# The first layer's output stage: one plain fp32 product in place of three fp32r passes

## What is computed

```python
rw = _gating(hidden_states, sim_matrix, gates)            # (4, 2048, 16)
q, k, v = ...                                             # weighed by rw, head width 64
attn = jnp.einsum('bqk,bkd->bqd', jax.nn.softmax(scores, axis=-1), v)
mixed = attn[:, :, None, :] * rw[..., None]               # (4, 2048, 16, 64)
return jnp.einsum('bted,edc->btc', mixed, o_proj)         # 16 * 64 = 1024 -> 256
...
x = _layernorm(x + _L0_ffn_ref(x, ...), axis=-1)
```

## Time and profile before

| | us |
|---|---|
| median of 3 runs | 3732.65 (3730.2 to 3733.83) |
| the profiled execution | 3733.13 |
| its span on the core | 3731.3 |

### The profile page before, as it was taken

One profiled execution on the slowest core, in us unless ns is written; L12 is line 12 of the kernel. 1 busy time (PEld: TensorE's weight loads), 2 busy tenths in 40 slices (PEclk: granted clock), 3 DMA queues, 4 the chain that ended last, 5 costly groups with the idle time before them and its releaser, 6 DMA issues. The chain is left out here.

```text
span 3731.3 us, 53569 instructions
## 1 busy us (share of the span) xinstructions
PE 3299.7 (88%) x19676; PEld 2562.2 (69%) x19676; DVE 2690.4 (72%) x4602; ACT 2018.3 (54%) x3256; POOL 1546.2 (41%) x765
## 2 busy tenths in 40 slices
PE   6898889998999889998888998888988889888877
PEld 2687758794778658783687745877558875488756
DVE  5676567654775567654899767997669985699948
ACT  4224232333224332324899547997379982799812
POOL 1100410031101310030699604997039980299915
PEclk9998999999999999998999999999999999999989
DMA  4000100001000200002111210112101122011230
GB/s 151 1 1 24 69 1 1 23 20 50 1 3 22 69 1 1 23 35 67 35 56 57 80 39 28 56 57 82 44 20 57 56 67 67 13 57 56 72 96 7
DMA packets 103563, 155.30 MB, mean 42 GB/s; under 512 B 15832, under 2 KB 54624, under 8 KB 101744
## 3 DMA queue, kind: packets, MB, share of 16 engines
q1 hardware_dynamic: 101552, 151.60, 12.6%
q10 hardware_dynamic: 1728, 0.02, 0.0%
HBM read 124.81 MB, written 26.78 MB: 41 GB/s over the span
## 5 line engine op out<-in xcount | busy, mean ns | idle before, releaser
L1720 POOL TENSOR_TENSOR hc<-h,c_sb 128x1024 f32<-128x1024 f32 x344 | 811.4, 2384 | 457.5 <-DVE h L1736 449.9
L1736 DVE TENSOR_TENSOR_SCAN h<-da,state,PS 128x512 f32<-128x512 f32 x768 | 902.2, 1257 | 18.7 <-PE PS L1605 13.5
L1605 PE MATMUL PS<-ident,tok 128*128 128x128 f32 x4032 | 598.6, 280 | 145.6 <-DVE h L1736 96.8
L1605 PEld LDWEIGHTS PS<-ident,tok 128*128 128x128 f32 x4032 | 453.5, 142 | 231.0 <-DVE h L1736 171.1
L1679 ACT ACTIVATE da<-dt,a_neg 128x2048 f32<-128x2048 f32 x252 | 505.9, 2008 | 20.7 <-issue 10.4
L1672 ACT ACTIVATE tok<-dtu,b_cols 128x512 f32<-128x512 f32 x768 | 492.4, 725 | 0.0
L1720 POOL TENSOR_TENSOR kept<-h,c_sb 128x1024 f32<-128x1024 f32 x168 | 400.9, 2386 | 3.3 <-PE PS L1630 3.3
L779 DVE SCALAR_TENSOR_TENSOR acc<-PS,rw,acc 128x192 f32<-128x192 f32 x768 | 283.6, 413 | 139.6 <-PE PS L697 75.9
L1624 PE MATMUL PS<-ident,hc 128*128 128x128 f32 x2752 | 357.3, 273 | 10.9 <-ACT dtu L1690 7.3
L122 POOL TENSOR_TENSOR ln_rstd<-ln_var,eps_pow 128x4 f32<-128x4 f32 x50 | 55.2, 1104 | 655.4 <-DVE ln_var L115 432.2
L1624 PEld LDWEIGHTS PS<-ident,hc 128*128 128x128 f32 x2752 | 310.1, 141 | 18.7 <-ACT dtu L1690 9.2
(11 more groups left out here) (277 smaller groups left out, 6144.6 us busy)
## 6 DMA issues: line engine op xcount, KB each, us to landing
c_sb<-bc_rows SPq DMA_DIRECT2D x256, 256.0 KB, 3.1
xT<-in_xT SPq DMA_DIRECT2D x5, 2048.0 KB, 7.6
tok<-in_x SPq DMA_DIRECT2D x4, 2048.0 KB, 9.5
x_after_layer<-tok SPq DMA_DIRECT2D x16, 512.0 KB, 2.9
xT_after_layer<-x2T_out SPq DMA_DIRECT2D x16, 512.0 KB, 2.7
tok<-x_after_layer SPq DMA_DIRECT2D x16, 512.0 KB, 5.4
out<-tok SPq DMA_DIRECT2D x16, 512.0 KB, 3.0
x2T<-xT_after_layer SPq DMA_DIRECT2D x12, 512.0 KB, 3.9
```

Source lines behind the costliest of these rows:

```text
L1605: op = pe.transpose(fill_bank(x)[:, c * P:(c + 1) * P], bt_at[s_ % 2][:, c, m * P:(m + 1) * P], ident[:, :])
L1720: pool.tensor_tensor(hc_at[p % 3], h[:, s_ % 2, 2 * j:2 * j + 2, :], c_sb[:, s_ % 3, :].unsqueeze(1).broadcast_to([P, 2, CHUNK]), ALU.mult)\
L1736: dve.tensor_tensor_scan(h[:, s_ % 2, m, :], da[:, s_ % 2, m, :], fill_bank(("b", s_, m)), first, ALU.mult, ALU.add).then_inc(sd, 1)
```

## The change

The activations and the output weights of this product stay plain fp32. The weights are loaded straight into `wo`, without ScalarE's rounding and VectorE's subtraction in the setup; the load is counted by the semaphore for which SyncE waits at the end of the setup. In the output stage ScalarE copies each transposed bank to `mixT`, VectorE's `low_parts` is gone, and the product has eight matmul instructions per tile in place of 24. `tc` is now signalled by ScalarE. The split of the other weights (`wmoh`) stays.

```diff
--- before.py
+++ after.py
@@ -177,7 +177,7 @@
         wqkvg = tile(L, "wqkvg", [P, KC, 4 * D])
         wout = tile(L, "wout", [P, KC, D])
         wmoh = [tile(L, "wmoh_" + part, [P, KC, EXPERTS * QKV], F32R) for part in ("hi", "lo")]
-        wo = [tile(L, "wo_" + part, [P, EXPERTS * EHD // P, D], F32R) for part in ("hi", "lo")]
+        wo = tile(L, "wo", [P, EXPERTS * EHD // P, D])
         bq = tile(L, "bq", [P, 4 * KC])
         bg_half = tile(L, "bg_half", [P, KC])
         bout = tile(L, "bout", [P, D])
@@ -207,11 +207,10 @@
             simr = tile(s, "simr", [P, EXPERTS])
             gts = tile(s, "gts", [P, EXPERTS])
             wmoh_in = tile(s, "wmoh_in", [P, KC, EXPERTS * QKV])
-            wo_in = tile(s, "wo_in", [P, EXPERTS * EHD // P, D])
             hi_ready = sem("wmoh_hi_ready")
             small, big, c_zero, c_mask = sem("small_loaded"), sem("big_loaded"), sem("pads_zero"), sem("mask_ready")
             stored = sem("x2_stored")
-            moh_in, wo_loaded = sem("wmoh_loaded"), sem("wo_loaded")
+            moh_in = sem("wmoh_loaded")
             iota_ready, a1, v1 = sem("iota_ready"), sem("setup_act"), sem("setup_dve")
             sq_ready = sem("squares_ready")
             pw, m1, kst, tl = sem("setup_pow"), sem("setup_mm"), sem("kernel_stored"), sem("toep_loaded")
@@ -225,7 +224,7 @@
                     sp.dma_start(gts[:, :], t["gates"].partition_broadcast(P)).then_inc(small, 16)
                     with nc.allow_non_contiguous_dma(reason="a bias, once"):
                         sp.dma_start(bq[:, :], t["bqkvg"].rearrange("(m p) -> p m", p=P)).then_inc(small, 16)
-                    for dst, name, loaded in ((wmoh_in, "Wmoh", moh_in), (wo_in, "Wo", wo_loaded), (wqkvg, "WqkvgT", big)):
+                    for dst, name, loaded in ((wmoh_in, "Wmoh", moh_in), (wo, "Wo", big), (wqkvg, "WqkvgT", big)):
                         sp.dma_start(dst[:, :, :], t[name].rearrange("(k p) n -> p k n", p=P)).then_inc(loaded, 16)
                     sp.wait_ge(v1, 6)
                     sp.dma_start(kpad, krow[:, :]).then_inc(kst, 16)
@@ -235,7 +234,7 @@
                     sp.wait_ge(kst, 16)
                     sp.dma_start(toep[:, :, :], bass.AP(tensor=kpad.tensor, offset=0,
                                                         ap=[[1, P], [640, HEADS], [1, FIELD]])).then_inc(tl, 16)
-                    sp.wait_ge(big, 16 * 4)
+                    sp.wait_ge(big, 16 * 5)
 
                 @block.gpsimd
                 def _(pool):
@@ -270,8 +269,6 @@
                     act.wait_ge(moh_in, 16)
                     for k in range(KC):
                         act.activation(wmoh[0][:, k, :], wmoh_in[:, k, :], ACT.Copy).then_inc(hi_ready, 1)
-                    act.wait_ge(wo_loaded, 16)
-                    act.activation(wo[0][:, :, :], wo_in[:, :, :], ACT.Copy).then_inc(hi_ready, 1)
 
                 @block.vector
                 def _(dve):
@@ -349,8 +346,6 @@
                     for k in range(KC):
                         dve.wait_ge(hi_ready, k + 1)
                         dve.tensor_tensor(wmoh[1][:, k, :], wmoh_in[:, k, :], wmoh[0][:, k, :].bitcast(F32), ALU.subtract)
-                    dve.wait_ge(hi_ready, KC + 1)
-                    dve.tensor_tensor(wo[1][:, :, :], wo_in[:, :, :], wo[0][:, :, :].bitcast(F32), ALU.subtract)
 
                 @block.tensor
                 def _(pe):
@@ -972,10 +967,9 @@
     with ExitStack() as g:
         x2T = tile(g, "x2T_out", [P, KC, SEQ])
         mix = tile(g, "mix", [P, 2, EXPERTS, EHD])
-        mix_hi, mix_lo = (tile(g, n, [P, 2, 8, P], F32R) for n in ("mix_hi", "mix_lo"))
-        mr, tr, th, tc, yr, yu = (sem(n) for n in (
-            "mix_ready", "mix_tr", "mix_hi_ready", "mix_lo_ready", "o_ready", "o_used"))
-        passes = [(x, part, k) for k in range(8) for x, part in ((mix_hi, 0), (mix_hi, 1), (mix_lo, 0))]
+        mixT = tile(g, "mixT", [P, 2, 8, P])
+        mr, tr, tc, yr, yu = (sem(n) for n in (
+            "mix_ready", "mix_tr", "mix_copied", "o_ready", "o_used"))
         ln2 = layer_norm("ln2", g, tok, x2T)
         with nc.Block() as block:
             @block.sync
@@ -1008,9 +1002,9 @@
                     pe.wait_ge(tc, 2 * i + 2)
                     if i >= 2:
                         pe.wait_ge(yu, i - 1)
-                    for q, (x, part, k) in enumerate(passes):
-                        last = pe.matmul(bank(4 + i % 2)[:, 0:D], x[:, i % 2, k, :], wo[part][:, k, :],
-                                         start=(q == 0), stop=(q == len(passes) - 1))
+                    for k in range(8):
+                        last = pe.matmul(bank(4 + i % 2)[:, 0:D], mixT[:, i % 2, k, :], wo[:, k, :],
+                                         start=(k == 0), stop=(k == 7))
                     last.then_inc(yr, 1)
 
                 for i in range(TILES):
@@ -1037,18 +1031,7 @@
                     dve.wait_ge(yr, i + 1)
                     dve.tensor_tensor(tok[:, i, :], tok[:, i, :], bank(4 + i % 2)[:, 0:D], ALU.add).then_inc(yu, 1)
 
-                def low_parts(i):
-                    for h in range(2):
-                        dve.wait_ge(th, 2 * i + h + 1)
-                        if i >= 2:
-                            dve.wait_ge(yr, i - 1)
-                        dve.tensor_tensor(mix_lo[:, i % 2, 4 * h:4 * h + 4, :],
-                                          bank(2 * (i % 2) + h).rearrange("p (k n) -> p k n", k=4),
-                                          mix_hi[:, i % 2, 4 * h:4 * h + 4, :].bitcast(F32), ALU.subtract)\
-                           .then_inc(tc, 1)
-
                 for i in range(TILES):
-                    low_parts(i)
                     if i:
                         add(i - 1)
                     if i and i % 4 == 0:
@@ -1074,9 +1057,9 @@
                         act.wait_ge(tr, 2 * i + h + 1)
                         if i >= 2:
                             act.wait_ge(yr, i - 1)
-                        act.activation(mix_hi[:, i % 2, 4 * h:4 * h + 4, :],
+                        act.activation(mixT[:, i % 2, 4 * h:4 * h + 4, :],
                                        bank(2 * (i % 2) + h).rearrange("p (k n) -> p k n", k=4),
-                                       ACT.Copy).then_inc(th, 1)
+                                       ACT.Copy).then_inc(tc, 1)
                     if i >= 9 and i % 4 == 1:
                         ln2.copy(act, (i - 9) // 4)
                 ln2.copy(act, 2)
```

## The result

| | us |
|---|---|
| changed kernel, median of 4 runs | 3758.56 (3756.57 to 3763.97) |
| kernel before, beside it | 3732.93 |
| ratio | 1.0072, 95% interval 1.0055 to 1.009 |
| profiled execution; its span | 3758.01; 3756.2 |

The change makes the kernel 25.6 us slower; 31.9 us were forecast, at 3764.5 us in a range of 3757 to 3771. In two later comparisons the ratio was 1.0071 (1.0058 to 1.0085) and 1.0073 (1.006 to 1.0087).

A forecast was written before the change was run, and what follows sets the result against it. TensorE alone was taken to bound the output stage. Products +37.2, scaling waits -3.3, setup -2.2 and stage start +0.2 summed to +31.9 us, giving 3764.5 us in a range of 3757 to 3771.

The forecast's parts named there:

- The bound: Output stage: TensorE alone sets the pace, busy 60.70 of 61.30 us in the first batch.
- The price of a plain product: Output stage: two records of 0.2156 us, 0.431 us against 0.3585 for three passes; +37.2 us over 64 tiles.
- Rivals A and B: Output stage: A, one record per plain product, 3666 us, chance 2%; B, four passes of 0.1195 us, 3789 us, 3%.
- The joints: Output stage, between transposes and products: might differ by 0.06 us either way per tile, +-3.8 us.
- The waits for the scaling: Tiles 9 and 13: TensorE's 0.42 us waits for VectorE's layer norm scaling go, -3.3 us, at worst 0.
- the setup: End of setup: without the weights' split the whole block moves up by 2.19 us, -2.2 us, at worst 0.
- The start of the stage: Output stage's first tile, at low clock: grows by about 0.62 instead of 0.58 us, +0.2 us over four batches.
- rival C: Output stage start: clock returns later under fewer, longer products, at most +11.2 us, 3776; chance of more than half 8%.

## Why the prediction was right

- **The bound.** TensorE alone sets the stage's pace, as read from the earlier trace rows: confirmed by the run without low parts, whose tiles keep their 3.74 us.
- **The price of a plain product.** Two records of 0.2156 us from the earlier trace rows: 4.33 us a tile against 4.325 forecast, and the run with half the slices gives 0.4325 per product. Rivals A and B fall by this. With the same 128x128 weights a plain record of 512 columns steps at 0.43 us, twice as far, so the step follows the columns and not the loading of the weights. The count of records in the earlier trace rows against the loops was the step that decided the sign.
- **The joints** cost nothing beyond the 0.875 us; the bound of 3.8 us either way wasn't needed.
- **The waits for the scaling** went (5.20 us between two tiles there, which is 4.33 + 0.87). They went because TensorE comes later, not because VectorE has less to do: without the low parts alone they stayed. And **the setup** gave 2.2 us, shown by putting the split back.
- **The start of the stage** was mis-sized: 0.2 us were forecast over four batches. From the transposes of tile 0 to those of tile 2 the first profile has 9.17, 7.73, 7.57 and 7.59 us against 6.94, 7.02, 7.03 and 7.11, 4.0 us in all where 2.5 follow from the forecast: 1.5 us more, nearly all in the first batch, where 5.55 us pass from the first product's start to the next transposes. That is what rival C describes, in one batch of four, but not its reason. I took the moment at which the clock comes back as fixed; it is not, and the longer products don't decide it. All three profiles of the changed kernel have the late clock in the first batch. The run with the split kept, whose output stage is the same, has 7.68 us there, and the second profile of the kernel before has a late clock in its last batch (8.38 us). With idle products the clock was 1.00 in all batches. The working has a slip besides: at half speed five records of the old product fit into the 1.20 us of the earlier trace rows, not six. Its 0.2 us follow from five; with six they would come out as -0.3.
- **The end of the stage** was held for unchanged and wasn't. From the first matmul of the last product to the last transposes pass 7.86 us in place of 7.64, where the longer product asked 0.58 more; 0.36 us less for each batch, 1.4 in all. The run without low parts shows 0.3 of it too, so it goes with their removal: the four aggregations of line 109 run in one go, 0.38 us, where they were broken by 0.17 us of issue. First the kernel before, then the run without low parts:

```profile
436.77 0.25 DVE L109 BATCH_NORM_AGGREGATE ln_mv<-ln_stats 128x2 f32<-128x6 f32 x2
437.19 0.25 DVE L109 BATCH_NORM_AGGREGATE ln_mv<-ln_stats 128x2 f32<-128x6 f32 x2 [0.17 <-issue]
```

```profile
435.65 0.38 DVE L109 BATCH_NORM_AGGREGATE ln_mv<-ln_stats 128x2 f32<-128x6 f32 x4
```

  And from the last transposes to the next stage pass 1.9 us less in sum, all in the last two batches, where those transposes ran at the full clock (1.09 in place of 1.97 us in the last). This isn't fixed by the change either: with the split kept they took 1.09 us in all four batches, with idle products at the stage's start 1.97 us in all four. What decides it is not tested.
- **The sum.** Output stages: 37.2 - 3.3 + 0.2 = 34.1 forecast, 30.6 to 32.5 measured; with the setup 28.4 to 30.2 us for 31.9. The medians show 25.6 to 27.0; the last 2 or 3 us lie within the 8 us by which the untouched stages differ between executions, and are not settled. The mechanism, the sign and the main terms came out as forecast. That the median lies 6 us below the forecast and still inside the range is in part luck: the low end was opened for the joints and the spread of the runs, the joints didn't need it, and it took in the 3.3 us at the end of the stage, which no term stood for, and what is not settled.

## What to carry to other kernels

Count the records that one instruction leaves in a neighbouring group of the same type before pricing a change of type: three rounded passes in place of one plain fp32 product were the cheaper form here, 0.3585 against 0.431 us for 256 columns. Work that is taken off an engine which the bound engine never waits for gives next to nothing; a subtraction that ends a block, so that all engines wait for it, gave 2.2 us. Before moving work to an idle GpSimd, look at what VectorE does beside it. And when two edits come in one run, the sums of the stages alone don't tell which edit gave what.

## What the runs showed of the hardware

- Beside an instruction of GpSimd on SBUF, several kinds of VectorE's instructions on SBUF last until GpSimd's has ended: one of 0.17 us took 4.46 (to 29.29, GpSimd's to 29.26), one of 0.69 took 9.17, four of 1.38 in sum took 4.20. It is not so for all. VectorE's low parts (line 1045), which read PSUM and SBUF, kept 679 to 694 ns beside GpSimd's mixes, and in the changed kernel a reduction kept 0.69 us beside the bias addition that held another instruction for 6.56:

```profile
48.01 8.85 POOL L416 TENSOR_TENSOR tok<-tok,bout 128x4096 f32<-128x4096 f32 x1 [13.08 <-DMA tok<-in_x]
48.53 0.69 DVE L558 TENSOR_REDUCE tail<-dep_late 128x1 f32<-128x512 f32 x1
50.85 6.56 DVE L572 SCALAR_TENSOR_TENSOR qf<-feat_tmp 128x512 f32<-128x512 f32 x1 [1.64 <-ACT feat_tmp L521]
```

  "SBUF — State Buffer" in the Trainium skill, section "SBUF: two separate sides", describes a port pair that the two engines share, locked for the whole instruction; the traces agree for the instructions that were held (29.29 and 29.26 above).
- The fp32r pass of 256 columns steps at 0.1195 us at full clock, and a plain fp32 record of the same shape at 0.2156, less than twice that. Why a plain record is quicker than two rounded passes was not tried.
- Idle products on TensorE at the start of the output stages kept the granted clock there at 1.00 in all four batches. Without them TensorE stood idle for 2.58 us ahead of the first transposes, and the mean over the starts was 0.66 to 0.79 in the rows of the changed kernel above and 0.69 in the earlier trace rows.
